# One block for four token tiles, and weight quantisation spread 6, 9, 9, 8 over them instead of 7, 10, 8, 7

## What is computed

```python
# layer 0
scores = (q @ k.T) * scale            # q, k, v: projections of xn
weights = exp(log_decay * dist) * causal   # only later tokens count
x = x + ((scores * weights) @ v) @ Wo.T * out_scale \
      + xn @ quantize_int4(kernel) + bias + (xn @ a) @ b
# layer 1
x = x + alpha * (decayed causal linear attention(xn)) @ W_read.T \
      + relu(xn @ quantize(W1).T + b1) @ quantize(W2).T + b2
# quantize(W) = clip(round(W / (mean|W| + eps)), -1, 1)
```

## Time and profile before

| | us |
|---|---|
| median of 2 runs | 1544.89 (1543.82 to 1545.97) |
| the profiled execution | 1543.28 |
| span of its slowest core, number 5 | 1541.7 |
| spans of the 8 cores | 1521.5 to 1541.7 |
| TensorE busy | 1234.5 (80% of the span) |
| ScalarE busy | 474.4 (31%) |
| VectorE busy | 418.5 (27%) |
| GpSimd busy | 136.1 (9%) |

### The profile page before, as it was taken

One profiled execution on the slowest core, in us unless ns is written; L12 is line 12 of the kernel. 1 busy time (PEld: TensorE's weight loads), 2 busy tenths in 40 slices (PEclk: granted clock), 3 DMA queues, 4 the chain that ended last, 5 costly groups with the idle time before them and its releaser, 6 DMA issues. The chain is left out here.

```text
span 1541.7 us, 15405 instructions; the slowest of 8 cores (1521.5 to 1541.7 us)
## 1 busy us (share of the span) xinstructions
PE 1234.5 (80%) x5440; PEld 532.4 (35%) x5440; DVE 418.5 (27%) x704; ACT 474.4 (31%) x550; POOL 136.1 (9%) x184
## 2 busy tenths in 40 slices
PE   0276179996699477794639999999997999999997
PEld 0022024442244132231214444444443444444443
DVE  0498345001323332433257400030002200041000
ACT  0564023334532753726113242014202140032400
POOL 2331100000110120212110000000000000000000
PEclk9999579998899798896869999999998999999999
DMA  9696773002344565747394352354235152252432
GB/s 200 105 168 112 104 114 56 1 1 82 110 116 166 170 199 181 212 151 233 127 161 85 136 143 83 131 191 139 83 134 191 31 154 88 84 191 71 121 109 109
DMA packets 74202, 194.42 MB, mean 126 GB/s; under 512 B 8272, under 2 KB 16496, under 8 KB 69776
## 3 DMA queue, kind: packets, MB, share of 16 engines
q0 software_dynamic: 37072, 105.34, 28.5%
q1 hardware_dynamic: 37056, 88.09, 18.2%
HBM read 195.57 MB, written 33.56 MB: 149 GB/s over the span
## 5 line engine op out<-in xcount | busy, mean ns | idle before, releaser
L1214 PE MATMUL pb<-bigA,wqA 128*128 128x512 bf16 x1024 | 226.2, 379 | 0.0
L1174 PE MATMUL pb<-xn,xbf 128*128 128x512 bf16 x1024 | 222.5, 380 | 0.3 <-DMA xbf<-W1qS 0.3
L1157 PE MATMUL pb<-stm,bigB 128*128 128x512 bf16 x640 | 148.0, 394 | 50.1 <-DVE xa_bf L1012 35.2
L1101 ACT ACTIVATE bigA<-pb,cstF 128x512 bf16<-128x512 f32 x128 | 99.7, 779 | 218.2 <-PE pb L1174 218.2
L1047 DVE SCALAR_TENSOR_TENSOR xf<-pb,cstF,xf 128x512 f32<-128x512 f32 x32 | 24.0, 750 | 480.0 <-PE pb L1214 480.0
L1196 PE MATMUL pb<-rt,projW 128*128 128x512 bf16 x512 | 126.0, 390 | 34.2 <-DVE rt L1017 29.7
L1174 PEld LDWEIGHTS pb<-xn,xbf 128*128 128x128 bf16 x1024 | 100.1, 98 | 122.2 <-issue 0.8
L1214 PEld LDWEIGHTS pb<-bigA,wqA 128*128 128x128 bf16 x1024 | 100.2, 98 | 120.8
L1157 PEld LDWEIGHTS pb<-stm,bigB 128*128 128x128 bf16 x640 | 63.5, 100 | 134.6 <-issue 65.9
L429 PE MATMUL pb<-rt,cstB 128*128 128x512 bf16 x112 | 32.6, 418 | 84.9 <-DVE rt L395 84.9
L1089 ACT ACTIVATE statsT<-xbf,cstF 128x1024 bf16<-128x1024 f32 x44 | 54.6, 1240 | 100.6 <-DMA xbf<-W2T 69.1
(11 more groups left out here) (129 smaller groups left out, 1108.3 us busy)
## 6 DMA issues: line engine op xcount, KB each, us to landing
wqA<-W2qS POOLq DMA_DIRECT2D x32, 1024.0 KB, 5.2
xbf<-W1qS SPq DMA_DIRECT2D x128, 256.0 KB, 2.6
xbf<-W2T SPq DMA_DIRECT2D x26, 512.0 KB, 4.1
xbf<-W1T SPq DMA_DIRECT2D x18, 512.0 KB, 4.5
bigA<-W2T POOLq DMA_DIRECT2D x32, 256.0 KB, 9.1
bigA<-W1T POOLq DMA_DIRECT2D x16, 512.0 KB, 9.6
xf<-xT SPq DMA_DIRECT2D x4, 2048.0 KB, 8.3
x1S<-xf POOLq DMA_DIRECT2D x4, 2048.0 KB, 7.9
```

The costliest lines, as they stand in the source:

```text
L1101: got = si(s.activation(bigA[:, fc * 512:(fc + 1) * 512], pb[fc % 2][:, :], AF.Relu, bias=biasL[:, 48 + fc:49 + fc], scale=sc[:, C_Q4:C_Q4 ...
L1157: got = ti(t.matmul(bank[:, :], bigB[:, i * 1024 + ec * 128: i * 1024 + (ec + 1) * 128], stm[:, i * 512:(i + 1) * 512], start=(n == 0), st ...
L1174: got = ti(t.matmul(bank[:, :], xbf[:, (fc % 4) * 1024 + dc * 128: (fc % 4) * 1024 + (dc + 1) * 128], xn[:, p0:p0 + TS], start=(dc == 0), ...
L1214: got = ti(t.matmul(bank[:, :], wqA[:, (dc % 2) * 4096 + fc * 128: (dc % 2) * 4096 + (fc + 1) * 128], bigA[:, fc * 512:(fc + 1) * 512], st ...
```

## The change

`QUC` goes from 7, 10, 8, 7 units to 6, 9, 9, 8. The tile loops of both layers put all four tiles into one block, so the barrier between tiles 1 and 2 goes, and tile 2 gets tile 1's tokens as `prev` instead of `None`. The waits that `prev` brings in tile 2 are the same as those of tiles 1 and 3 before.

```diff
--- before.py
+++ after.py
@@ -798,7 +798,7 @@
             prefA.append(v0 + tot)
         totalA = tot
         if layer == 0:
-            QUC = [7, 10, 8, 7]
+            QUC = [6, 9, 9, 8]
             u0 = sum(QUC[:j])
             units_j = list(range(u0, u0 + QUC[j]))
             NH = 2 * len(units_j)
@@ -1252,7 +1252,7 @@
                     t_R=t_R, t_res=t_res,
                     t_h=(t_h if layer == 1 else None), NS=NS)
 
-    for jp in ((0, 1), (2, 3)):
+    for jp in ((0, 1, 2, 3),):
         with nc.Block() as blk:
             prevt = None
             for j in jp:
```

## The result

The changed kernel takes 1537.29 us (median of 20 runs), the kernel before 1544.53 us (19 runs on the same chip). The ratio is 0.9948, with a 95% interval of 0.9935 to 0.9960, which is 8.0 us faster (6.2 to 10.0). The ratio leaves disturbed runs out, of which the median of 20 still holds some (up to 1722.74 us). The forecast was 1532 us, 12.9 less than before, in a range of 1523 to 1541. So the direction and the range hold, and about 5 us of the forecast gain did not come.

What follows compares the result with a forecast made beforehand. TensorE, busy 80%, was taken as the bound, its layer 0 waits set by quantisation steps ahead of R7. 1543.28 - 13.0 (layer 1) + 0.1 (layer 0) = 1530.4, plus 1.6 to the median: 1532 us, range 1523 to 1541.

Steps and rivals of the forecast that it cites:

- Layer 1, boundary: Between tiles 1 and 2 of layer 1: -13.0 us, 10.4 of idle time and 2.6 of low clock.
- Rival (c): Layer 1 gains nothing, the wait reappearing before line 1174 on W1 slabs queued behind xf; 1545 us, chance 0.05.
- Layer 0, tiles 0 and 1: Fewer quantisation steps ahead of R7: -2.7 us in tile 0, -7.9 us at the end of tile 1.
- Layer 0, boundary: Between tiles 1 and 2: idle time moves from before st to before R; store, reload, load, Sign gain only -2.6 us.
- Rival (a): Both boundaries pay: layer 0's is worth -12.6 us instead of -2.6; 1522 us, chance 0.11.
- the part of -1.1: Layer 0 boundary: store of x1S to reload of xf shrinks from 8.64 to 7.55 us, as inside a block.
- The rule of the Trainium skill on GpSimd's descriptors: Layer 0 boundary: VectorE's two-port operations block GpSimd's DMA descriptors, delaying the store; at worst 2.6 us higher forecast.
- Layer 0, tile 2: 12 instead of 10 quantisation steps ahead of R7: +7.5, and +0.4 for denser steps, together +7.9 us.
- Tile 3: Layer 0: 9 instead of 8 quantisation steps ahead of R7, 719.38 to 722.06, costing +2.7 us.
- rival (b): Layer 0, tiles 2 and 3: quantisation pace worsens from 3.32 to 4.13 us a step; 1547 us, chance 0.06.
- R's wait of "about 17 us": Sign of being right: in layer 0's tile 2, R's wait for xa_bf grows from 3.29 to about 17 us.
- 5 us or more from 723.35: Sign of being wrong: layer 0's tile 3 projection starts that far from its old time, expected unchanged.

Runs made afterwards that it cites:

- e3: The kernel before with only layer 1 merged into one block, QUC still 7, 10, 8, 7; 1534.17 us, ratio 0.9919 to the kernel before.
- e1: The changed kernel (both layers merged) with the old QUC 7, 10, 8, 7; 1530.82 us, ratio 0.9910 to the kernel before.
- e4: The kernel before with only layer 0 merged into one block, QUC still 7, 10, 8, 7; 1543.81 us, ratio 0.9990 to the kernel before.
- e2: The kernel before with only the new QUC 6, 9, 9, 8, both layers in blocks of two tiles; 1545.76 us, ratio 1.0008.
- e6: Changed kernel with old QUC, SyncE issuing layer 0's first quantisation loads before waiting for x1S's store and reloading xf; 1506.46 us, ratio 0.9767 to the kernel before.

## Why the prediction was right, step by step, and where it was off

**Layer 1, boundary: forecast -13.0, measured -12.5 (e3, timed), -12.9 (table) and -13.02 (core 5).** Each part came as written: next group after 6.91 us, clock 1.00, R 22.08 us after `st` where 22.06 was worked out. Rival (c), a wait on W1 slabs in front of line 1174, is out.

**Layer 0, tiles 0 and 1: forecast -2.7 and -7.9 at the end of tile 1, measured -3.5 and -8.6** (table, from tile 0's start). The q's that moved behind R7 were hidden in the projection phase: 32.9 us from tile 1's projection to tile 2's start.

**Layer 0, boundary: forecast -2.6, measured -1.3 to -1.5 timed** (e1 against e3, e4 against before, both no more than the intervals allow by chance), -1.0 to -2.0 in the table (the same pairs, from tile 1's projection to tile 2's). The idle time went from in front of `st` to in front of R, as forecast. Rival (a), 1522 us, is out: e4 shows 1.5 us and not 12.6. The sum of two parts was mis-sized. GpSimd's store of `x1S` and SyncE's reload of `xf` after, on core 5 (answers to the earlier trace rows):

```profile
573.14 0.89 POOL L166 DMA_DIRECT2D x1S<-xf  x1 [8.55 <-DVE biascols L985]
```

```profile
581.58 0.38 SPq L166 DMA_DIRECT2D xf<-xT  x1
```

Store to reload is 8.44 us, not the 7.55 of inside a block that I took; across the boundary it was 8.64. Over the eight cores the median here is 8.3 us after (7.5 to 8.6) and 8.2 before. So the part of -1.1 didn't come: the barrier had little to do with it. Why this store takes longer than that of tile 0 (7.55 in both) stays open. From the reload to the first Sign, 591.23 below, it is 9.65 us, where 9.59 was taken: that part came on this core (11.08 before), and by half in the median over the cores (10.2 before, 9.6 after). The rule of the Trainium skill on GpSimd's descriptors (SBUF — State Buffer, the "DVE blocks DMA" trap) isn't seen at work. The issue takes 0.89 us with VectorE busy beside it, as it did with VectorE idle, and store to reload is 8.44 and 8.64 us.

**Layer 0, tile 2: forecast +7.9, measured +7.3** (changed kernel against e1, 61.3 against 54.0; in pairs, e2 against before, 5.2). **Tile 3: forecast +2.7, measured +4.7** (49.3 against 44.6; in pairs 4.6). Tile 3's is the term that was most off. First Signs of the q's after, on ScalarE (answers to the earlier trace rows): tile 2's 1st, 5th, 9th and 12th, and tile 3's 5th, 8th and 9th:

```profile
591.23 1.24 ACT L1089 ACTIVATE statsT<-xbf,cstF 128x1024 bf16<-128x1024 f32 x1 [13.21 <-DMA xbf<-W2T]
...
603.16 1.24 ACT L1089 ACTIVATE statsT<-xbf,cstF 128x1024 bf16<-128x1024 f32 x1
...
617.94 1.24 ACT L1089 ACTIVATE statsT<-xbf,cstF 128x1024 bf16<-128x1024 f32 x1
...
628.72 1.24 ACT L1089 ACTIVATE statsT<-stm,cstF 128x1024 bf16<-128x1024 f32 x1 [1.58 <-DVE rt L1017]
...
697.67 1.24 ACT L1089 ACTIVATE statsT<-xbf,cstF 128x1024 bf16<-128x1024 f32 x1 [2.82 <-DMA xbf<-W1T]
...
706.11 1.24 ACT L1089 ACTIVATE statsT<-stm,cstF 128x1024 bf16<-128x1024 f32 x1
712.62 1.24 ACT L1089 ACTIVATE statsT<-xbf,cstF 128x1024 bf16<-128x1024 f32 x1 [4.13 <-DMA xbf<-W1T]
```

The pace of tile 2 is (628.72 - 591.23) / 11 = 3.41, near the 3.32 of before, so rival (b), a worse pace, is out. But the steps don't come evenly. Four slots go round in 11.93 and 14.78 us here, and a single step takes from 2.5 us, where its load has landed, to 5.1, where ScalarE waits for it. Tile 3's ninth step is one of the long ones. It comes 6.51 us after the eighth on this core, and 4.2 in the median over the cores (2.5 to 6.5; 4.2 in e1 too). The forecast took 722.06 - 719.38 = 2.7 from core 5 in the earlier trace rows, one interval from one core of one execution; the eight cores of that trace have 2.5 to 4.5, median 3.0. So reading all cores would have given 0.3 us more, and the rest of the miss is that the step itself was longer in the changed kernel. Why it was stays open.

**The sum.** Layer 0 was forecast at +0.1 and is +3.2 in the table (351.4 against 348.2). Layer 1 is -12.9. The last projection comes 10.3 us earlier, counted from tile 0's start, where 12.9 were forecast. Put by parts of the change, the forecast has -15.6 for the two boundaries and +2.7 for `QUC` (-7.9 + 7.9 + 2.7); timed, the boundaries gave -13.8 (e1), and `QUC` cost 5.8 behind merged blocks and 1.2 in pairs (e2). So the gain fell short by about 2 us at the boundaries and 3 in `QUC`. The timed gain is 8.0 (6.2 to 10.0) and that between the two profiled executions 8.8; the last 2 us between trace and timing are not explained. One slip of the prediction: the bounds that it gives for its terms (-0.3 to +2.6, -0.4 to +2.6, 2 either way) add up to 1529 to 1539 about 1532, not to 1527 to 1538. The measured 1537.29 lies in both, near the upper end.

Of the signs named in advance, the clock and the missing idle time in layer 1, R's wait of "about 17 us" (17.29) and the first Sign of tile 2 (18.09 us after the store, not under 15) came out right. One spoke against the forecast: tile 3's projection was to start at the same time. From tile 0's start it comes 354.95 - 348.00 = 6.9 us later on core 5, and 3.3 in the median. By its letter the sign "5 us or more from 723.35" was met (716.59), but as a time from the span's start it says nothing, since the tile 0 start had moved by 13.7.

## What to carry to other kernels

Idle time at a barrier is a gain only where nothing else is late behind it: follow the engine past the barrier to its next wait, and if that wait hangs on another chain (here store, reload, load, Sign), find what starts that chain. In an in-order queue a load whose buffer is free belongs ahead of one that has to wait; moving two lines in that way gave 22 us where the two changes under study gave 8. The pace of work that goes through a few slots is a mean: the ninth step of tile 3 took 2.5 to 6.5 us over the cores where a step of tile 2 takes 3.4 in the mean, so the price of one more step is read from many cores, not from one interval.

## What the runs showed of the hardware beside that

Transfers that now overlap got slower themselves. The median from issue to landing (out<-in, queue, operation, count, KB each, us), from the kernel after:

```profile
xf<-xT SPq DMA_DIRECT2D x4, 2048.0 KB, 8.2
...
stm<-W1T SPq DMA_DIRECT2D x16, 512.0 KB, 5.6
```

and from e6, where they overlap:

```profile
xf<-xT SPq DMA_DIRECT2D x4, 2048.0 KB, 11.0
...
stm<-W1T SPq DMA_DIRECT2D x14, 512.0 KB, 6.8
```

So e6 pays 2.8 us on a reload and 1.2 on one of these loads, at the median, and still gains. Loads of other places changed less (`xbf<-W1T` 4.9 to 5.5 us, `xbf<-W2T` 4.1 to 3.9). No run separates what of it comes from the core's own transfers and what from those of the other cores.
